# Attention: exchanging neighbouring partitions by transfers in place of two projections, and a later place for the tail's transposes, affinity and ranks

## The chip, the core and the metric

One core of one Trainium2 chip. The time is device microseconds for one execution of the whole program. The engines are PE (TensorE), ACT (ScalarE), DVE (VectorE), POOL (GpSimd) and SP (SyncE, which here only issues transfers). Each runs its own list of instructions in order; they meet at semaphores.

## The reference

The program is a chain of four layers over x [32, 256, 128]: attention with an MLP, a routed mixture of 8 experts, a selective scan and a rotation network. Only the first is touched. Cut to what matters (D = 128, 16 heads of 8):

```python
xn = _layernorm(x, ln1_g, ln1_b)
q = _l2norm((xn @ Wq).reshape(Bx, Tx, H, Dh))
k = _l2norm((xn @ Wk).reshape(Bx, Tx, H, Dh))
...
q = _rope(q, times)      # pairs: r1 = x1*cos - x2*sin, r2 = x1*sin + x2*cos
k = _rope(k, times)
gcp = jnp.exp(jnp.clip(jnp.cumsum(gj, axis=1), -60.0, 50.0))
q = q * gcp
k = k / (gcp + 1e-08)
...                      # p_exp, its cumulative sum p_cs
q = q / (p_cs + 1e-08)
k = k * p_exp
scores = jnp.einsum('bqhd,bkhd->bhqk', q, k) / math.sqrt(Dh)
attn = jax.nn.softmax(jnp.where(mask, scores, -jnp.inf), axis=-1)
...
# next layer's routing
aff = x @ centroids.T
eid = jnp.argmax(aff, axis=-1)
```

## The kernel before

Attention works on two sequences (512 tokens) at a time, 16 pairs, in software-pipelined steps k = -1 to 18. In one step four pairs are in flight: the layer norm of pair k+1 (`ln`), the projections of pair k (`front`), scores and softmax of pair k-1 (`scores`, its last quads `late` in the next step), and the MLP, routing and storing of older pairs (`mid`, `tail`). `tail` begins with step 3, `front` ends with step 15. The order of all work on each engine is written out by hand in `pe_step`, `act_step`, `dve_step`, `pool_step` and `sp_step`; nothing is reordered at run time.

*Projections.* Activations lie transposed, features on partitions, 512 tokens along the free axis. `project` is one fp32 product of 128x128 weights with `xt` into PSUM bank FA or FB. The rotary embedding needs each feature's neighbour (partition 2i with 2i+1). The kernel gets it by projecting a second time with the columns of the weights exchanged: `w_qs` beside `w_q`, `w_ks` beside `w_k`. DVE multiplies the one with `cos` (L812, L866), the other with `sin`, whose sign alternates by partition (L819, L861, into `rot_b`), and adds (L826, L918). The squares' sum over a head is a product with `ones_blk` (L481 for the query, L519 for the key).

*Scores.* `quad(n)` writes the scores of 4 heads into the four banks of RING, which exist once; it waits until `exps(n-1)` on ACT has read them. `exps(n)` writes `es`, which `weigh(n)` multiplies with V into the bank AV. `av_copy(i)` (ACT), `back(i)` (PE transposes), `heads_rec` and `heads_o` (DVE, L735 and L747) take each pair of weighs away:

```python
since(pe, s["s_exp"], u * 8 + n)        # in quad: RING is free
...
pe.wait_ge(s["s_exp"], u * 8 + n + 1)   # in weigh: es is there
```

*Tail.* DVE makes `xl2` (L762, four instructions) from the finished rows; PE transposes it (L352) into bank M, ACT copies it to `o_t` (L673), PE multiplies with the centroids (L507, the affinity), DVE derives the one-hot choice `hot`, and PE counts ranks from it (L535, L538) into FA, from which DVE takes `pos` and the slots. POOL scatters the rows. Bank M also serves the MLP.

*Clip and softplus.* POOL makes two products for the clock's softplus (L985 `f_lost`, L987 `f_soft`); DVE makes the cumulative sum `cum` (a scan, L858) and clips it (L863); ACT's `lgcp` (L679) needs the clip.

Of the kernel before, what the change touches and what calls it, by code (L numbers as in the profile page):

```python
# [80 lines left out]
def program(nc, dram, out):  # L81

    ctx = ExitStack()
    with ctx:
# [40 lines left out]
        for name, shape in (("w_a", [P, dram["w_a"].shape[1]]), ("w_1", [P, E * F]), ("w_2", [P, E * F])):  # L125
            c[name] = layer0.enter_context(nc.sbuf_tensor(name, shape, fp32))
# [10 lines left out]
        for name, width in W_A:  # L137
            c[name] = c["w_a"][:, at:at + width]
            at += width
# [28 lines left out]
def attention(nc, dram, d, c, banks):  # L168
# [18 lines left out]
    with ExitStack() as ctx:  # L187
# [4 lines left out]
            f_q f_qs f_sq f_ra f_rb f_rq f_ssq f_mq f_lq f_zq f_zq2 f_fq f_qt  # L192
            f_k f_ks f_sk f_ka f_kb f_rk f_ssk f_mk f_lk f_zk f_fk f_k1 f_k2 f_km f_v f_vaug
# [33 lines left out]
        rot_b = sb("rot_b", [P, STEP])  # L227
        factor = sb("factor", [P, STEP])
# [47 lines left out]
        of = sb("of", [1, ETILES])  # L276
        before = sb("before", [1, ETILES])
# [40 lines left out]

        def sp_step(sp, k, half, p, ln, front, scores, late, mid, tail):
# [18 lines left out]
            if front:  # L338

                sp.wait_ge(s["f_xlb"], one_on)  # L340
                sp.dma_start(rows(d["xlb"], here), xl[:, :, :]).then_inc(s["xlb_stored"], 16)


        def pe_step(pe, k, half, p, ln, front, scores, late, mid, tail):
# [171 lines left out]
            if front:  # L516
                pe.wait_ge(s["f_ka"], k + 1)
                pe.wait_ge(s["f_sk"], k + 1)
                pe.matmul(FB[:, :], c["ones_blk"], square[:, :], start=True, stop=True).then_inc(s["f_ssk"], 1)  # L519
            if scores:  # L520
                quad(3, k - 1, q)
            if mid:
# [5 lines left out]
                transposes(M, o_tok[p], s["m_ot"])  # L528
            if tail:
                pe.wait_ge(s["r_hot"], k - 2)  # L530
                if front:
                    pe.wait_ge(s["f_kb"], k + 1)
# [9 lines left out]
            if scores:  # L542
                weigh(2, k - 1, q)
                quad(4, k - 1, q)
# [9 lines left out]
            if front:  # L554
                pe.wait_ge(s["f_kb"], k + 1)
# [8 lines left out]
        def act_step(act, k, half, p, ln, front, scores, late, mid, tail):  # L564
# [106 lines left out]
            if tail:  # L671
                act.wait_ge(s["m_x2t"], k - 2)
                act.activation(o_t[:, :], M[:, :], ACT.Copy).then_inc(s["m_x2t_sb"], 1)  # L673
# [6 lines left out]
            if scores:  # L680
                av_copy(0, k - 1)
                exps(2, k - 1)
            if front:
# [40 lines left out]
        def dve_step(dve, k, half, p, ln, front, scores, late, mid, tail):  # L724
# [1930 lines left out]
```

## Time and profile before

| | |
|---|---|
| median of 3 runs | 2163.32 us (2157.25 to 2165.94) |
| the profiled execution, its span | 2164.4 us |
| attention, from the start of the span | about 780 us |
| PE busy in the span | 1849.2 us |
| DVE busy | 1703.8 us |
| ACT busy | 1474.7 us |
| POOL busy | 1165.1 us |

The span runs from the first to the last instruction of one profiled execution; no other time of that execution is on record, so the span stands for it. Busy times are of the whole program, whose later layers have other limits, so a step of attention has to be read in a timeline of its own.

### The profile page before, as it was taken

What the parts mean: (1) busy time and instruction counts of PE and PEld (TensorE: products, weight loads), DVE (VectorE), ACT (ScalarE), POOL (GpSimd) and SP (SyncE); (2) the same over time, 40 slices, a digit from 0 to 9 for tenths busy, and PEclk for the clock granted to TensorE, in tenths of its full rate; (3) what the DMA queues carried; (4) which work ended last, traced back from release to release, by engine and by line L of the source; (5) the groups of instructions that cost most, each with busy time, mean ns of one, the idle gap of its engine ahead of it and who ended that gap; (6) DMA issues with size and microseconds to landing.
All of it is one profiled execution on the core that took longest, in us unless ns stands there. A gap on an engine that the chain in (4) does not pass through costs nothing. (4 is left out here: it accounts for less than half of the span.)

```text
span 2164.4 us, 37241 instructions
## 1 busy us (share of the span) xinstructions
PE 1849.2 (85%) x12576; PEld 954.5 (44%) x12600; DVE 1703.8 (79%) x3547; ACT 1474.7 (68%) x2917; POOL 1165.1 (54%) x720
## 2 busy tenths in 40 slices
PE   6999999999998459957889889898898988659996
PEld 2566666656665259952222222222222222124453
DVE  7778868877863437854899999999999998976776
ACT  5888888888885138845656666666666666437775
POOL 2122232242221027871789999999999998840001
PEclk9999999999999669977899999999999998879998
DMA  4100010011001012221100111001111100023333
GB/s 169 36 26 26 28 49 26 26 36 41 21 25 33 20 50 77 88 72 42 30 25 27 34 35 34 27 30 30 31 35 35 35 31 30 21 67 90 97 84 78
DMA packets 103708, 97.35 MB, mean 45 GB/s; under 512 B 9137, under 2 KB 86113, under 8 KB 103137
## 3 DMA queue, kind: packets, MB, share of 16 engines
q1 hardware_dynamic: 95584, 75.34, 12.4%
q0 software_dynamic: 6784, 18.10, 2.5%
q8 instruction: 103, 1.69, 0.3%
q10 hardware_dynamic: 1152, 1.54, 0.2%
q14 instruction: 85, 0.69, 0.1%
HBM read 45.87 MB, written 28.10 MB: 34 GB/s over the span
## 5 line engine op out<-in xcount | busy, mean ns | idle before, releaser
L1935 POOL TENSOR_TENSOR hc<-h,c_rep 128x1024 f32<-128x1024 f32 x256 | 627.8, 2463 | 137.9 <-DVE h L1899 136.7
L1899 DVE TENSOR_TENSOR_SCAN h<-decay,bank 128x1024 f32<-128x1024 f32 x241 | 551.0, 2286 | 22.5 <-issue 0.9
L1757 ACT ACTIVATE decay<-bank,neg_a_r 128x510 f32<-128x510 f32 x512 | 322.6, 683 | 257.5 <-PE bank L1634 257.1
L1618 PE MATMUL bank<-u_in,sel_rows 32*128 32x512 f32 x964 | 287.9, 675 | 95.7 <-DVE h L1899 95.6
L1634 PE MATMUL bank<-delta,sel_rows 32*128 32x512 f32 x1024 | 338.8, 677 | 0.9 <-ACT decay L1757 0.9
L1886 DVE TENSOR_TENSOR bank<-bank,b_rep 128x1024 f32<-128x1024 f32 x241 | 291.2, 1208 | 34.8 <-PE bank L1618 33.0
L992 POOL DMA_INDIRECT rows_in_dram<-row,idx x64 | 63.3, 989 | 318.3 <-DVE row L965 303.7
L574 ACT ACTIVATE es<-bank 128x384 f32<-128x384 f32 x512 | 208.9, 499 | 22.1 <-PE bank L373 21.8
L1618 PEld LDWEIGHTS bank<-u_in,sel_rows 32*128 32x128 f32 x964 | 76.0, 191 | 276.7 <-DVE h L1899 199.7
L1649 PE MATMUL bank<-hc,y_sel 128*32 128x512 f32 x1024 | 149.6, 660 | 0.8 <-POOL hc L1935 0.8
L1656 PE MATMUL bank<-xpad,w_conv 128*128 128x512 f32 x256 | 133.0, 634 | 3.2 <-ACT xc L1819 1.6
L985 POOL TENSOR_TENSOR mag<-mag,front 128x512 f32<-128x512 f32 x16 | 21.4, 1335 | 194.6 <-ACT front L660 194.6
L2546 POOL DMA_DIRECT2D out_dram<-r_res x16 | 12.1, 759 | 209.9 <-DVE r_res L2413 202.0
L348 PE MATMUL bank<-xt,w_a 128*128 128x512 f32 x224 | 117.1, 608 | 7.9 <-DVE lnorm L915 3.8
L1634 PEld LDWEIGHTS bank<-delta,sel_rows 32*128 32x128 f32 x1024 | 99.9, 193 | 25.1 <-ACT decay L1757 18.2
L365 PE MATMUL bank<-q_t,k_m 32*128 32x256 f32 x1024 | 91.9, 428 | 2.3 <-ACT es L574 2.1
L387 PE MATMUL bank<-es,v_a 128*32 128x256 f32 x1024 | 81.4, 388 | 9.2 <-DVE o_tok L747 7.9
L418 PE MATMUL bank<-h_t,w_a 128*128 128x512 f32 x128 | 77.6, 690 | 13.1 <-ACT g L584 7.5
L1656 PEld LDWEIGHTS bank<-xpad,w_conv 128*128 128x128 f32 x256 | 43.2, 192 | 89.6 <-issue 83.6
L1350 POOL DMA_INDIRECT yx_dram<-yx,e_idx x72 | 70.2, 974 | 19.6 <-issue 16.4
L1299 PE MATMUL bank<-w,hid 128*128 x576 | 80.3, 283 | 0.0
L1287 PE MATMUL bank<-xst,w_tile 128*128 128x128 f32 x576 | 77.8, 279 | 1.7 <-issue 0.4
(341 smaller groups left out, 4170.0 us busy)
## 6 DMA issues: line engine op xcount, KB each, us to landing
r_tw<-r_o_t SPq DMA_DIRECT2D x96, 128.0 KB, 2.3
xvs<-xv SPq DMA_DIRECT2D x16, 512.0 KB, 2.9
u_wide<-u_rep_dram SPq DMA_DIRECT2D x30, 256.0 KB, 3.5
xs<-rows_in_dram SPq DMA_DIRECT2D x72, 68.0 KB, 1.8
front<-in_x_dram SPq DMA_DIRECT2D x16, 256.0 KB, 2.9
w<-in_w_dram SPq DMA_DIRECT2D x2, 2048.0 KB
xlb_dram<-front SPq DMA_DIRECT2D x16, 256.0 KB, 2.3
xlb_m<-xlb_dram SPq DMA_DIRECT2D x16, 256.0 KB
```

Source lines behind the costliest of these rows:

```text
L348: pe.matmul(bank[:, :], weight, xt[p][:, :], start=True, stop=True).then_inc(sem, 1)
L365: pe.matmul(RING[st][:, 0:T], kk[:, 0:P], qq, start=True, stop=True, tile_position=(32 * st, 0))
L387: pe.matmul(dst[:, col:col + T], v_a[par][:, 2 * b, HS * st + v, :], e[:, 0:T], start=True, stop=True, tile_position=(0, 32 * st))
L574: last = act.activation(es[(n % 2) * HS + st][:, :], RING[st][:, 0:3 * P], ACT.Exp, scale=DH ** -0.5)
L1618: last = pe.matmul(BD[n % 2][:, i * STEP:(i + 1) * STEP], sel[at:at + 32, r, :], u_in[p if n < NS else q][at:at + 32, hf, :], start=True, ...
L1634: pe.matmul(DL[i], sel[at:at + 32, r, :], delta[p if n < NS else q][at:at + 32, hf, :], start=True, stop=True, tile_position=(at, 0)).then ...
L1649: last = pe.matmul(Y[32 * st:32 * st + 32, :], c["y_sel"][:, r, :], hc[(2 * i + st // 2) % RING][:, st % 2, :], start=False, stop=r == 3, ...
L1656: last = pe.matmul(seq(G), c["w_conv"][:, tap, hf * P:(hf + 1) * P], xpad[:, :, tap:tap + T], start=tap == 0, stop=tap == TAPS - 1)
L1757: act.activation(decay[n % 4][:, i, :, 1:], seq(DL[i])[:, :, 1:], ACT.Exp, scale=c["neg_a_r"][:, hf, g:g + 1]).then_inc(s["n_da"], 1)
L1886: dve.tensor_tensor(pair_of(BD[n % 2]), pair_of(BD[n % 2]), b_rep[p if n < NS else q][:, :].unsqueeze(1).to_broadcast([P, 2, STEP]), ALU.m ...
L1899: dve.tensor_tensor_scan(flat(h[n % RING]), decay[n % 4].rearrange("p i b t -> p (i b t)"), flat(drive_0) if by_pool else BD[n % 2], 0.0, ...
L1935: pool.tensor_tensor(hc[n % RING][:, :, :], h[n % RING][:, :, :], c_rep[p if n < NS else q][:, :].unsqueeze(1).to_broadcast([P, 2, STEP]), ...
```

## The change

`w_qs` and `w_ks` and their two projections go. DVE multiplies the one projection with `cos` and with `sin`; the product with `sin` (`rot_b`) is then copied to `rot_s` with each pair of partitions exchanged, by two transfers of 64 partitions x 2 KB on SP's queue. As the alternating sign is taken before the exchange, the sum becomes a subtraction. The key's copy is ordered behind the query's (one `rot_s`). On DVE the query's subtraction moves from behind `centred(h_tok)` to behind `f_sp`, the key's product with `sin` to behind that with `cos`. On PE the query's `ones_blk` product moves between `weigh(6)` and `weigh(7)`, the key's projection behind `quad(0)`, the transposes of `xl2` behind `quad(2)`, the affinity behind the key's `ones_blk` product, the ranks behind `quad(4)`. On ACT the copy `o_t` of the transposes moves behind `exps(2)`. On DVE the work on `aff` and `hot` forms one run behind `heads_o(0)`, `pos` moves behind `q_t`. POOL's `f_lost` additionally waits for `m_xl2`. The weights `w_a` are loaded in three pieces without the two left out.

```diff
+        def swap(sp, sem):
+
+            for to in range(2):
+                sp.dma_start(rot_s[to:P:2, :], rot_b[1 - to:P:2, :]).then_inc(sem, 16)
...
# sp_step
             if front:
 
+                sp.wait_ge(s["f_rb"], one_on)
+                swap(sp, s["f_qsw"])
+                sp.wait_ge(s["f_kb"], one_on)
+                sp.wait_ge(s["f_rq"], one_on)
+                swap(sp, s["f_ksw"])
                 sp.wait_ge(s["f_xlb"], one_on)
...
# pe_step
             if late:
                 quad(7, k - 2, p)
-            if front:
-                pe.wait_ge(s["f_pe"], k + 1)
-                project(FB, c["w_qs"], s["f_qs"])
             if late:
                 weigh(6, k - 2, p)
+            if front:
+                pe.wait_ge(s["f_sq"], k + 1)
+                pe.wait_ge(s["f_rb"], k + 1)
+                pe.matmul(FA[:, :], c["ones_blk"], square[:, :], start=True, stop=True).then_inc(s["f_ssq"], 1)
+            if late:
                 weigh(7, k - 2, p)
...
                 quad(0, k - 1, q)
+            if front:
+                pe.wait_ge(s["f_pe"], k + 1)
+                project(FB, c["w_k"], s["f_k"])
             if late:
                 back(3, k - 2)
-            if front:
-                pe.wait_ge(s["f_sq"], k + 1)
-                pe.wait_ge(s["f_ra"], k + 1)
-                pe.matmul(FA[:, :], c["ones_blk"], square[:, :], start=True, stop=True).then_inc(s["f_ssq"], 1)
-                pe.wait_ge(s["f_rb"], k + 1)
-                project(FB, c["w_k"], s["f_k"])
...
-            if front:
-                pe.wait_ge(s["f_mq"], k + 1)
-                project(FA, c["w_ks"], s["f_ks"])
             if scores:
                 weigh(0, k - 1, q)
+            if scores:
+                weigh(1, k - 1, q)
+                quad(2, k - 1, q)
             if tail:
                 pe.wait_ge(s["m_xl2"], k - 2)
                 if ln:
                     pe.wait_ge(s["f_xt_sb"], k + 2)
                 transposes(M, xl2, s["m_x2t"])
-            if scores:
-                weigh(1, k - 1, q)
-                quad(2, k - 1, q)
-            if tail:
-                pe.wait_ge(s["m_x2t_sb"], k - 2)
-                for j in range(TS):
-                    last = pe.matmul(M[:, j * E:(j + 1) * E], o_t[:, j * P:(j + 1) * P], c["cent"][:, :], start=True, stop=True)
-                last.then_inc(s["m_aff"], 1)
             if scores:
                 back(0, k - 1)
...
             if front:
-                pe.wait_ge(s["f_ka"], k + 1)
+                pe.wait_ge(s["f_kb"], k + 1)
                 pe.wait_ge(s["f_sk"], k + 1)
                 pe.matmul(FB[:, :], c["ones_blk"], square[:, :], start=True, stop=True).then_inc(s["f_ssk"], 1)
+            if tail:
+                pe.wait_ge(s["m_x2t_sb"], k - 2)
+                for j in range(TS):
+                    last = pe.matmul(M[:, j * E:(j + 1) * E], o_t[:, j * P:(j + 1) * P], c["cent"][:, :], start=True, stop=True)
+                last.then_inc(s["m_aff"], 1)
             if scores:
                 quad(3, k - 1, q)
...
# the ranks (L535, L538) stand behind this now, no longer ahead of it
             if scores:
                 weigh(2, k - 1, q)
                 quad(4, k - 1, q)
...
# act_step
             if scores:
                 av_copy(0, k - 1)
                 exps(2, k - 1)
+            if tail:
+                act.wait_ge(s["m_x2t"], k - 2)
+                act.activation(o_t[:, :], M[:, :], ACT.Copy).then_inc(s["m_x2t_sb"], 1)
...
# dve_step
                 dve.tensor_tensor(seq(rot), seq(FA), cos, ALU.mult).then_inc(s["f_ra"], 1)
+                since(dve, s["f_ksw"], 32 * k)
+                dve.tensor_tensor(seq(rot_b), seq(FA), sin, ALU.mult).then_inc(s["f_rb"], 1)
...
                 dve.scalar_tensor_tensor(pre[:, 0, :], pre[:, 0, :], 0.0, log[:, 0, :], ALU.max, ALU.add).then_inc(s["f_sp"], 1)
+                dve.wait_ge(s["f_ra"], k + 1)
+                dve.wait_ge(s["f_qsw"], 32 * k + 32)
+                dve.tensor_tensor(rot[:, :], rot[:, :], rot_s[:, :], ALU.subtract).then_inc(s["f_rq"], 1)
...
                 dve.tensor_tensor(seq(rot_k), seq(FB), cos, ALU.mult).then_inc(s["f_ka"], 1)
+                dve.wait_ge(s["f_qsw"], 32 * k + 32)
+                dve.tensor_tensor(seq(rot_b), seq(FB), sin, ALU.mult).then_inc(s["f_kb"], 1)
...
+                dve.wait_ge(s["f_ksw"], 32 * k + 32)
+                dve.tensor_tensor(rot_k[:, :], rot_k[:, :], rot_s[:, :], ALU.subtract).then_inc(s["f_rk"], 1)
...
# pool_step
                 pool.wait_ge(s["f_back"], k + 1)
+                if tail:
+                    pool.wait_ge(s["m_xl2"], k - 2)
                 pool.tensor_tensor(mag[:, 1, :], mag[:, 1, :], one_up[:, :], ALU.subtract).then_inc(s["f_lost"], 1)
```

## Rows read from the trace of the kernel before

**Rows 1.** The page's busy times; the window view of one pass (length, then busy us).

```profile
PE 1849.2 (85%) x12576; PEld 954.5 (44%) x12600; DVE 1703.8 (79%) x3547; ACT 1474.7 (68%) x2917; POOL 1165.1 (54%) x720
...
310.60:352.40 41.80, 39.86 (x409) 26.23 (x408) 32.34 (x114) 36.04 (x78) 12.59 (x11) 1.00 0.11 33
```

**Rows 2.** Timeline of PE: start, length, line, operation, count, idle time before it.

```profile
294.51 0.66 PE L352 MATMUL bank<-consts,xl 128*128 128x128 f32 x4 [1.05 <-DVE xl L762]
...
325.77 1.02 PE L348 MATMUL bank<-xt,w_a 128*128 128x512 f32 x2
326.73 0.64 PE L387 MATMUL bank<-es,v_a 128*32 128x256 f32 x8
...
327.40 0.61 PE L387 MATMUL bank<-es,v_a 128*32 128x256 f32 x8
...
336.34 0.66 PE L352 MATMUL bank<-consts,xl 128*128 128x128 f32 x4 [1.05 <-DVE xl L762]
336.93 0.64 PE L387 MATMUL bank<-es,v_a 128*32 128x256 f32 x8
...
337.71 0.71 PE L365 MATMUL bank<-q_t,k_m 32*128 32x256 f32 x8
...
339.03 0.96 PE L507 MATMUL bank<-cent,o_t 128*128 128x8 f32 x8
...
341.27 0.71 PE L365 MATMUL bank<-q_t,k_m 32*128 32x256 f32 x8
...
343.16 0.19 PE L535 MATMUL bank<-hot,strict_b 128*128 128x32 bf16 x1
...
344.16 0.71 PE L365 MATMUL bank<-q_t,k_m 32*128 32x256 f32 x8
```

**Rows 3.** Timeline of ACT in the same pass: L580 is `av_copy`, L574 `exps`.

```profile
328.46 0.58 ACT L580 ACTIVATE avs<-bank 128x512 f32<-128x512 f32 x1
...
329.98 1.62 ACT L574 ACTIVATE es<-bank 128x384 f32<-128x384 f32 x4
...
333.56 1.62 ACT L574 ACTIVATE es<-bank 128x384 f32<-128x384 f32 x4
...
339.38 1.62 ACT L574 ACTIVATE es<-bank 128x384 f32<-128x384 f32 x4
...
342.45 1.64 ACT L574 ACTIVATE es<-bank 128x384 f32<-128x384 f32 x4 [0.27 <-PE bank L373]
```

**Rows 4.** Timeline of DVE in the same pass.

```profile
326.75 0.17 DVE L757 BATCH_NORM_AGGREGATE m_mean_var<-m_stats 128x2 f32<-128x6 f32 x1
...
327.04 0.66 DVE L819 TENSOR_TENSOR rot_b<-bank,consts 128x512 f32<-128x512 f32 x1
...
331.20 0.23 DVE L735 RECIPROCAL rec<-bank 128x16 f32<-128x16 f32 x1
...
333.01 3.28 DVE L762 TENSOR_SCALAR xl<-row,m_mean_var 128x128 f32<-128x128 f32 x4
...
337.92 0.41 DVE L863 TENSOR_SCALAR cum<-cum 128x512 f32<-128x512 f32 x1
```

**Rows 5.** Timeline of POOL in the same pass.

```profile
333.06 1.27 POOL L985 TENSOR_TENSOR mag<-mag,front 128x512 f32<-128x512 f32 x1 [11.72 <-ACT front L660]
```

**Rows 6.** Timeline of DVE in step 16, where POOL has no such product.

```profile
666.35 1.11 DVE L762 TENSOR_SCALAR xl<-row,m_mean_var 128x128 f32<-128x128 f32 x4
```

**Rows 7.** Timelines of DVE and of POOL in step 2.

```profile
82.97 1.23 DVE L858 TENSOR_TENSOR_SCAN cum<-consts,pre 128x512 f32<-128x512 f32 x1
...
85.81 1.10 DVE L863 TENSOR_SCALAR cum<-cum 128x512 f32<-128x512 f32 x1
...
83.38 1.88 POOL L985 TENSOR_TENSOR mag<-mag,front 128x512 f32<-128x512 f32 x1 [22.40 <-ACT front L660]
85.34 1.29 POOL L987 TENSOR_TENSOR log<-log,mag 128x512 f32<-128x512 f32 x1
```

**Rows 8.** Transfers of the last stage by line: issue us min/median/max, then time to landing.

```profile
L2103 SPq DMA_DIRECT2D r_tw<-r_o_t x48: 588/597/1064, 1946.5 to 2136.7; - x48
...
DMA to landing us min/median/max: 2.3/2.4/4.0
```

More of the change, by code:

```diff
@@ L124, in program @@
         layer0 = ctx.enter_context(ExitStack())
-        for name, shape in (("w_a", [P, dram["w_a"].shape[1]]), ("w_1", [P, E * F]), ("w_2", [P, E * F])):
+        for name, shape in (("w_a", [P, dram["w_a"].shape[1] - 2 * D]), ("w_1", [P, E * F]), ("w_2", [P, E * F])):
             c[name] = layer0.enter_context(nc.sbuf_tensor(name, shape, fp32))
@@ L227, in attention @@
         rot_b = sb("rot_b", [P, STEP])
+        rot_s = sb("rot_s", [P, STEP])
         factor = sb("factor", [P, STEP])
@@ L275, in attention @@
         end = sb("end", [1, E])
-        of = sb("of", [1, ETILES])
-        before = sb("before", [1, ETILES])
+        of, before = (log[0:1, 0, n * ETILES:(n + 1) * ETILES] for n in range(2))
         hi = sb("p_hi", [E * FC, P], bf16)
@@ L528, in pe_step @@
                 transposes(M, o_tok[p], s["m_ot"])
+            if scores:
+                weigh(2, k - 1, q)
+                quad(4, k - 1, q)
             if tail:
@@ L541, in pe_step @@
                 last.then_inc(s["r_rank"], 1)
-            if scores:
-                weigh(2, k - 1, q)
-                quad(4, k - 1, q)
             if mid:
@@ L815, in dve_step @@
                 bn_aggr(mv_m, stats_m, s["m_mv2"])
-            if front:
-                dve.wait_ge(s["f_qs"], k + 1)
-                since(dve, s["f_rk"], k)
-                dve.tensor_tensor(seq(rot_b), seq(FB), sin, ALU.mult).then_inc(s["f_rb"], 1)
             if tail:
@@ L822, in dve_step @@
                 centred(h_tok, x2, mv_m, rs_m, s["m_yn"])
-            if front:
-                dve.wait_ge(s["f_ra"], k + 1)
-                dve.wait_ge(s["f_rb"], k + 1)
-                dve.tensor_tensor(rot[:, :], rot[:, :], rot_b[:, :], ALU.add).then_inc(s["f_rq"], 1)
             if tail:
@@ L889, in dve_step @@
                 dve.scalar_tensor_tensor(factor[:, :], lnorm[:, :], -0.5, cum[:, :], ALU.mult, ALU.subtract).then_inc(s["f_zq"], 1)
+            if scores:
+                heads_o(0, k - 1, q)
+            if tail:
+                dve.wait_ge(s["m_aff"], k - 2)
+                dve.tensor_copy(aff[:, :, :], M[:, 0:TS * E].rearrange("p (j e) -> p j e", j=TS)).then_inc(s["m_aff_sb"], 1)
+                dve.wait_ge(s["m_aff_sb"], k - 2)
+                dve.tensor_reduce(best[:, :], aff[:, :, :], AX.X, ALU.max).then_inc(s["r_dve"], 1)
+            if tail:
+                dve.wait_ge(s["r_dve"], 9 * k - 26)
+                dve.tensor_tensor(hot_f[:, :, :], aff[:, :, :], best[:, :].unsqueeze(2).to_broadcast([P, TS, E]), ALU.is_ge).then_inc(s["r_dve"], 1)
             if tail:
@@ L896, in dve_step @@
                 dve.tensor_reduce(first[:, :], hot_f[:, :, :], AX.X, ALU.max).then_inc(s["r_dve"], 1)
-            if scores:
-                heads_o(0, k - 1, q)
             if tail:
@@ L906, in dve_step @@
                 dve.tensor_tensor(factor[:, :], factor[:, :], pcs[:, :], ALU.subtract).then_inc(s["f_zq2"], 1)
+            if front:
+                dve.wait_ge(s["f_ssk"], k + 1)
+                dve.wait_ge(s["f_zq"], k + 1)
+                dve.tensor_scalar(lnorm[:, :], FB[:, :], 1e-24, None, ALU.max).then_inc(s["f_mk"], 1)
+                dve.wait_ge(s["f_ka"], k + 1)
+                dve.wait_ge(s["f_ksw"], 32 * k + 32)
+                dve.tensor_tensor(rot_k[:, :], rot_k[:, :], rot_s[:, :], ALU.subtract).then_inc(s["f_rk"], 1)
+                dve.wait_ge(s["f_fq"], k + 1)
+                dve.wait_ge(s["f_rq"], k + 1)
+                since(dve, s["s_score"], 32 * k - 32)
+                dve.tensor_tensor(q_t[p][:, :], rot[:, :], factor[:, :], ALU.mult).then_inc(s["f_qt"], 1)
             if tail:
@@ L984, in pool_step @@
                 pool.wait_ge(s["f_back"], k + 1)
+                if tail:
+                    pool.wait_ge(s["m_xl2"], k - 2)
                 pool.tensor_tensor(mag[:, 1, :], mag[:, 1, :], one_up[:, :], ALU.subtract).then_inc(s["f_lost"], 1)
```

48 lines of the change are left out of this document (13 added, 35 removed).

## The prediction

> **What bounds the kernel now.** I read the page first: TensorE (PE) is the busiest engine of the whole span [rows 1]. The change touches only attention, so the second view is the timeline of one steady pass there. Its landmark, the four transposes of `xl2`, comes at 294.51 and again at 336.34 [rows 2]: a pass takes 41.83 us, and the thirteen passes from step 3 to step 15 repeat it to 0.01 us. In it PE is busy 39.86 us, ACT 36.04, DVE 32.34 [rows 1]. So PE looks like the bound, with one visible hole of 1.05 us where it waits for DVE's `xl2` [rows 2]. The obvious sum is then two projections (0.96 us each, 325.77 to 326.73) and that hole, 2.97 us a pass.
>
> The rows say that this is not the whole chain. PE is in lockstep with ACT: `quad(n)` may not overwrite RING before `exps(n-1)` has read it, and `weigh(n)` needs `exps(n)`. A quad's scores release `exps` 1.18 us after the quad starts (341.27 to 342.45) and `exps` takes 1.62 to 1.64 us; `exps(3)` ends at 342.45 + 1.64 = 344.09 and `quad(4)` starts at 344.16 [rows 2, 3]. A quad can start only some 2.89 us after the one before, whatever PE is spared. So I follow the pass of 320 to 352 piece by piece, both engines and DVE, in the order of the changed code. Work that is not named keeps its durations.
>
> **Step 1, the query's projection goes and its normaliser comes early.** `quad(7)` ends at 325.77. Now `weigh(6)` follows 0.96 us earlier, to 326.44. Next in PE's queue is the `ones_blk` product, which now waits for `f_rb`. DVE's `rot_b` starts at 327.04 today, behind the aggregate of 326.75 [rows 4]; in its new place ahead of it, it starts at 326.75 and ends 0.66 later, at 327.41. PE stalls 1.02 us, the product takes about 0.90 (an estimate just under a projection of the same shape), and `weigh(7)` starts at 328.36 where it was at 327.40 [rows 2]: +0.96. Behind it on ACT is `av_copy(3)`, in order, at 328.46 [rows 3] and now, when `weigh(7)` has ended, at 329.25 (an estimate: its 0.78 and a hand-over); `exps(0)` follows 1.52 behind as today, from 329.98 to 330.77, +0.79. The removed projection has bought a stall of its own size, and the product that was moved is the delay. `quad(1)` has to wait for `exps(0)`: 330.77 + 1.64 + 0.07 = 332.48.
>
> **Step 2, the key's projection goes.** ACT runs without a gap from `exps(0)` to `exps(1)`, 3.58 us (329.98 to 333.56) [rows 3], so `exps(1)` starts at 334.36 and ends at 335.98. PE now has nothing between `weigh(0)` and `weigh(1)` and stands 1.55 us, until 336.05. `weigh(1)` takes 0.78 (336.93 to 337.71), then `quad(2)` starts at 336.83, was 337.71 [rows 2]: here 0.88 us is ahead.
>
> **Step 3, DVE, POOL and the port.** `back(3)` now stands behind the key projection, so DVE's `rec` moves from 331.20 to 331.98 [rows 4] (+0.78), and the query's sum `rot - rot_s`, moved behind it, adds 0.60. `xl2` starts at 333.01 + 1.38 = 334.39. Today it takes 3.28 us, since POOL's `f_lost` product starts 0.05 us later and runs beside it [rows 4, 5]; where POOL is idle the same four take 1.11 [rows 6]. POOL will now wait for `m_xl2`, so it ends at 335.50, 0.79 earlier. But the two POOL products then start just as DVE's scan `cum` starts. Steps 0 to 2 show that collision: the scan at 82.97 ran 1.23 to 84.20, the POOL product issued at 83.38 lasted 1.88 and ended 1.06 behind the scan, and the clip, issued at 85.81 beside the second POOL product, ended 0.28 behind that (86.91) instead of after 0.41 [rows 7]. In the new pass: scan 335.43 to 336.66, first POOL product to 337.72, clip to 338.00. Without the collision the clip would end at 337.1. It ends at 338.33 today [rows 4], so 0.33 is left of the gain. It feeds ACT's `lgcp`, which stands in front of `av_copy(0)` and `exps(2)`: `exps(2)` from 339.38 to 339.05 [rows 3], ending 340.67.
>
> The page "SBUF — State Buffer" of the Trainium skill, section "Who interferes with whom", has a rule for this: a DVE instruction with two SBUF inputs, or in a 2-port mode, and a GpSimd instruction that reads SBUF exclude each other, the first to start holding the pair to its end. It speaks against the change: by it the collision is certain, and the forecast's sum holds; without it the sum would be that of the rival "no collision" below. The trace agrees in steps 0 to 2 and shows nothing of it for this pair in the steady pass.
>
> **Step 4, the tail's transposes, affinity and ranks.** The `xl2` transposes no longer wait. Their copy `o_t` now follows `exps(2)` on ACT: 340.53 to 341.11 (a 128x512 copy takes 0.58 [rows 3]). The affinity needs it and starts at 341.16; it takes 0.96 [rows 2], of which some 0.15 lies beside the next instruction (an estimate), and `quad(3)` starts at 341.97, was 341.27: +0.70. So the affinity, formerly ahead, now stands in the lockstep. `exps(3)` 343.15 to 344.79, `quad(4)` 344.86 (+0.70). The ranks now come behind it, 0.22 (343.16 to 344.16 less `weigh(2)`'s 0.78) [rows 2]; before they filled the wait for `exps(3)`. `quad(5)` is late by 0.9, then `exps(5)`, `k_m` and `h_t`, which are in that order on ACT, and through `h_t` the next pass. DVE's part (`hot` now in one dependent run, `pos` behind the ranks) ends about 1 us late too and holds `weigh(4)`, but the next pass is set by ACT's +0.9.
>
> **Step 5, the four transfers a pass.** SP's other four issues of a pass wait for `f_xn`, `m_x1`, `m_y1` and `f_xlb`, none of which falls due between the swaps and their users, so the queue is free (where `xlb_dram` is stored late, POOL alone waits for it). Nearest row: the 128 KB twists of the last stage, 0.60 us of issue and 2.4 us to landing [rows 8], two in a row about 3 us after the operand is ready. The query's is ready at 327.41 and wanted at 333.71; the key's at 339.16 and wanted at 344.92. Each has some 3 us to spare: cost nothing; each microsecond of landing beyond 5.7 would cost one. The stride of two partitions is not in the trace; I bound a transfer between 2.4 and its longest there, 4.0 [rows 8], and both hide. The weights come in three pieces instead of one at the start, hidden behind the constants. DVE's count of large instructions is unchanged.
>
> **Sum.** 13 steady passes (3 to 15) at +0.9: 11.7. Step 16 has no projections and no transfers, but the affinity behind `exps(2)`: +1.3. Steps 0 to 2 have no `xl2`; the late `rot - rot_s` moves the scan from before to behind POOL's product, and step 0 also waits for its transfer: I take an estimate of +1.0 each, between 0 and +2 (the clip's 0.7 lost to a collision today [rows 7], once or twice more): 3. Together +16.0 on the profiled execution, whose trace spans 2164.4 us; that is 1.1 above the median of the three runs, which becomes 2163.3 + 16.0 = 2179 us.
>
> **The rivals.**
> *As worked out*, 2179: chance 0.50. Its own range, from the neglected hand-over times (0.05 to 0.1 each, some six in the chain, so ±0.5 a pass), is 2171 to 2188.
> *No collision*: scan and POOL product run side by side. `exps(2)` starts at 338.1, the copy and affinity make it `quad(3)` at 341.1, 0.2 early, and the ranks take it back: 0.0 a pass, +4 in all, 2167. For it: rows 7 are of other passes. Against it: they are the same two instructions. 0.22.
> *PE is the bound after all*, the other side: ACT's order gives way and the stalls before `ones_blk` (1.02) and `weigh(1)` (1.55) do not appear. Then 2.97 a pass is saved, 39 us, 2124. For it: PE's 39.86 of 41.8. Against it: `exps(0)` to `exps(1)` has no gap on ACT. It decides if PE's idle time a pass falls below the present 2 us. 0.12, with cases halfway (2145).
> *POOL takes the port first*: its semaphore comes 0.05 us behind a scan that starts 0.07 before `xl2` ends. If POOL wins, the scan waits a whole product, the clip comes 1.2 later still: +2.1 a pass, 27 + 4.3, 2195. 0.10.
> *A swap lands late*, from 5.7 us on: at 7 us +1.3 more a pass, 2196. 0.06.
>
> **How the numbers follow.** A measurement of this kernel tells about 0.5% from no change, 10.8 us: below 2152.5 is faster, above 2174.1 slower. Slower: most of the first (0.44) and of the last two (0.15), 0.59 together. Same: 0.06 of the first, 0.18 of "no collision", 0.03 elsewhere, 0.27. Faster: 0.11 and a strip of "no collision", 0.14. The range reaches from 2150, leaving out most of the third case, to 2197, which holds the last two where they just begin: 0.15 to 0.2 outside.
>
> **What would show it.** Right: PE idle of about 1.0 before the first `ones_blk` product and 1.5 before `weigh(1)`; busy PE down by 1.9 to about 38 and a pass of 42.7; `xl2` in 1.1 us; POOL's first product near 2.2 us and a clip of 1.3; `quad(3)` behind the affinity; no DVE wait on `rot_s`. Wrong: a pass under 41.8, a clip of 0.41, or DVE idle at `rot - rot_s`. The forecast falls if ACT reaches `exps(1)` sooner after `exps(0)` than 3.58 us, or if `quad(3)` is not held by the affinity.

## The result, and the profile after

| | before | changed |
|---|---|---|
| median of 4 runs each | 2162.13 us | 2191.73 us (2185.43 to 2197.31) |
| span of the profiled execution | 2164.4 us | 2195.5 us |
| a steady pass | 41.83 us | 43.19 us |
| start of the experts' stage | 784.78 us | 812.78 us |

The ratio is 1.014 with an interval of 1.0118 to 1.0161: slower, on the predicted side and in the range, but by 30 us where 16 were forecast. All but 3 us of the 31 by which the two spans differ has arisen when the experts' stage starts, so it lies in attention.

I followed one landmark there, the start of the down-projection (L460 before, L472 after): steps 0 to 2 cost 9.7 us (step 3 has it at 121.22, was 111.52), thirteen passes cost 1.36 each, 17.6, step 16 costs 1.3, and the rest gives back 0.6. Together 28.0. The two terms that are far off are the first (forecast 3) and the second (forecast 11.7).

The page's busy times, and the window of one pass as in [rows 1] (length, then busy of PE, its weight loads, DVE, ACT, POOL):

```profile
PE 1840.4 (84%) x12536; PEld 948.6 (43%) x12536; DVE 1701.4 (77%) x3547; ACT 1475.8 (67%) x2917; POOL 1176.5 (54%) x720
...
337.17:380.36 43.19, 38.91 (x403) 25.66 (x403) 31.97 (x113) 36.13 (x78) 13.42 (x12) 1.00 0.14 44
```

PE is busy 0.95 us less in a pass and the pass is 1.36 us longer; DVE and ACT are about as busy as they were. The granted clock is 1.00 in both windows, the upper level of 2.4 GHz. So the pass is not longer by more work: somebody waits. PE's timeline of that pass, against [rows 2]:

```profile
344.05 1.10 PE L482 MATMUL bank<-square,consts 128*128 128x512 f32 x2 [0.84 <-DVE rot_b L822]
345.07 0.64 PE L399 MATMUL bank<-es,v_a 128*32 128x256 f32 x8
...
352.69 0.64 PE L399 MATMUL bank<-es,v_a 128*32 128x256 f32 x8 [1.22 <-ACT es L582]
...
353.48 0.71 PE L377 MATMUL bank<-q_t,k_m 32*128 32x256 f32 x8
...
354.80 0.60 PE L364 MATMUL bank<-consts,xl 128*128 128x128 f32 x4
...
357.93 1.06 PE L526 MATMUL bank<-cent,o_t 128*128 128x8 f32 x8 [0.49 <-ACT o_t L690]
358.92 0.71 PE L377 MATMUL bank<-q_t,k_m 32*128 32x256 f32 x8
...
361.79 0.71 PE L377 MATMUL bank<-q_t,k_m 32*128 32x256 f32 x8 [0.17 <-ACT es L582]
...
363.11 0.18 PE L546 MATMUL bank<-hot,strict_b 128*128 128x32 bf16 x1
```

The old wait of 1.05 before the `xl2` transposes (L364) is gone. In its stead PE waits for `rot_b` before the `ones_blk` product, for `es` before `weigh(1)`, and for `o_t` before the affinity. ACT, as in [rows 3]:

```profile
346.00 0.60 ACT L588 ACTIVATE avs<-bank 128x512 f32<-128x512 f32 x1 [0.38 <-PE bank L403]
...
347.53 1.62 ACT L582 ACTIVATE es<-bank 128x384 f32<-128x384 f32 x4
...
351.02 1.62 ACT L582 ACTIVATE es<-bank 128x384 f32<-128x384 f32 x4
...
354.75 0.63 ACT L684 ACTIVATE lgcp<-cum 128x512 f32<-128x512 f32 x1 [1.10 <-DVE cum L865]
...
355.76 1.62 ACT L582 ACTIVATE es<-bank 128x384 f32<-128x384 f32 x4
357.25 0.63 ACT L690 ACTIVATE o_t<-bank 128x512 f32<-128x512 f32 x1
...
360.10 1.64 ACT L582 ACTIVATE es<-bank 128x384 f32<-128x384 f32 x4 [0.88 <-PE bank L385]
```

From `exps(0)` to `exps(1)` it still has no gap (3.49 us). DVE, as in [rows 4]:

```profile
343.22 0.68 DVE L822 TENSOR_TENSOR rot_b<-bank,consts 128x512 f32<-128x512 f32 x1
...
344.71 1.11 DVE L770 TENSOR_SCALAR h_tok<-x,m_mean_var,m_rstd 128x128 f32<-128x128 f32 x4 [0.51 <-ACT m_rstd L641]
...
348.68 0.26 DVE L743 RECIPROCAL rec<-bank 128x16 f32<-128x16 f32 x1 [0.80 <-PE bank L411]
...
350.44 0.69 DVE L853 TENSOR_TENSOR rot<-rot,rot_s 128x512 f32<-128x512 f32 x1
...
351.12 1.11 DVE L770 TENSOR_SCALAR xl<-row,m_mean_var 128x128 f32<-128x128 f32 x4
352.14 1.22 DVE L863 TENSOR_TENSOR_SCAN cum<-consts,pre 128x512 f32<-128x512 f32 x1
353.40 1.32 DVE L865 TENSOR_SCALAR cum<-cum 128x512 f32<-128x512 f32 x1
```

and POOL, as in [rows 5]:

```profile
352.37 2.06 POOL L990 TENSOR_TENSOR mag<-mag,front 128x512 f32<-128x512 f32 x1 [14.49 <-DVE xl L770]
```

`xl2` takes 1.11 instead of 3.28, and the collision has moved to the scan, POOL's product and the clip, which takes 1.32 instead of 0.41. The sum `rot - rot_s` does not wait. The transfers of `rot_s`, by line, as in [rows 8]:

```profile
L324 SPq DMA_DIRECT2D rot_s<-rot_b x64: 464/564/989, 23.0 to 658.8; - x64
...
  DVE rot L853: 0.2, 1
...
DMA to landing us min/median/max: 1.9/2.1/3.8
```

In 64 transfers DVE waited once, for 0.2 us.

### The profile page after: what moved, and what is told of

Same layout as the page of the kernel before. It is cut to its first block and busy times, and to the rows that moved or that the text cites. A ratio compares the mean times of both kernels' runs of the same rounds, so it can differ in the third digit from the quotient of the medians.

```text
span 2195.5 us, 37201 instructions
## 1 busy us (share of the span) xinstructions
PE 1840.4 (84%) x12536; PEld 948.6 (43%) x12536; DVE 1701.4 (77%) x3547; ACT 1475.8 (67%) x2917; POOL 1176.5 (54%) x720
## 5 line engine op out<-in xcount | busy, mean ns | idle before, releaser
L990 POOL TENSOR_TENSOR mag<-mag,front 128x512 f32<-128x512 f32 x16 | 30.9, 1931 | 235.2 <-DVE xl L770 187.2
L360 PE MATMUL bank<-xt,w_a 128*128 128x512 f32 x160 | 85.7, 624 | 5.5 <-ACT v_a L601 3.3
L385 PE MATMUL bank<-mask_b,ident_b 128*128 128x256 bf16 x512 | 79.0, 277 | 0.0
```

Source lines behind the costliest of these rows:

```text
L360: pe.matmul(bank[:, :], weight, xt[p][:, :], start=True, stop=True).then_inc(sem, 1)
```

## The experiments

A pass is told as the distance of two down-projections in the steady stretch. The first four kernels ran on one chip; a second chip took the next four and a third the last four. On those two the ten passes from step 4 to step 13 are some 1.45 us longer than on the first, at one place that has nothing to do with the edits (last section); the pass told is that of these steps. So passes are compared within a chip: the changed kernel has 43.19 us in its first measurement (whose chip is not on record, but the kernel with the projections back has the same 43.19 on the first) and 44.67 on the third. It was not run on the second; there the kernel with doubled transfers, at 44.66, is taken for it (reasons below). Ratios are to the kernel before on the same chip.

**PE's time handed back.** The two projections return as products that nobody reads, at their old places in PE's order; the rest is the changed kernel.

```diff
             if late:
                 quad(7, k - 2, p)
+            if front:
+                pe.wait_ge(s["f_pe"], k + 1)
+                pe.matmul(FB[:, :], c["w_q"], xt[p][:, :], start=True, stop=True)
...
                 quad(1, k - 1, q)
+            if front:
+                pe.wait_ge(s["f_mq"], k + 1)
+                pe.matmul(FA[:, :], c["w_k"], xt[p][:, :], start=True, stop=True)
```

> The changed kernel with two projections of the size of those removed (128x512) put back at their old places on PE, with no reader: one behind quad(7), one behind quad(1). Theory A (the changed pass is set by waits for f_rb, exps(1) and the clip, so TensorE time there is worth nothing): both lie in PE's waits, 0.84 us in front of the ones_blk product and 1.22 in front of weigh(1); the pass stays at 43.19 us within 0.15 and the time within 0.2% of the changed kernel. Rival B (PE is the bound, and removing the projections did save): 1.9 us a pass more, +25 to +30 us.

Measured: 2192.46 us, ratio 1.0149 (1.0109 to 1.0188), pass 43.19. PE is 21 us busier over the whole and not a hundredth of a steady pass is lost: the wait before `ones_blk` is gone, that before `weigh(1)` shrank to 0.36. In this order, what the change takes off PE is worth nothing. PE's busy time in a pass is 40.62 here, where the same work had 39.86 before the change.

**The tail's work back.** The `xl2` transposes, the affinity and the ranks on PE, the copy `o_t` on ACT, and DVE's `aff`, `hot` and `pos` go back to their old places; exchange, `ones_blk` and key projection stay.

> The changed kernel with the tail's transposes, affinity, ranks, the copy o_t and DVE's small steps at the places of the kernel before; the transfers stay. Theory A (the affinity behind exps(2), 0.98 us, and the ranks, 0.2, stand in the lockstep of quads and exps): quad(3) goes back to directly behind exps(2), about 1.45 us earlier, the pass falls from 43.19 to 41.6 to 41.9 us, the time by 17 to 21 us, back to within 0.5% of the kernel before. Rival B (the exchange by transfers is what costs): the pass stays above 42.8. Rival C: the xl2 wait of 1 us comes back and eats half, pass 42.5.

Measured: 2176.93, ratio 1.0086 (1.0057 to 1.0115), pass 42.40. The late tail costs 0.79 a pass, more than half of the loss, but the pass didn't fall to the 41.6 to 41.9 of theory A; it lies nearest to rival C (42.5), whose wait for `xl2` is there. DVE has no gap behind `rec(3)` here, and PE now waits 0.81 for `xl2` and 0.85 for `hot`:

```profile
341.61 1.10 PE L482 MATMUL bank<-square,consts 128*128 128x512 f32 x2 [0.84 <-DVE rot_b L822]
...
349.84 0.66 PE L364 MATMUL bank<-consts,xl 128*128 128x128 f32 x4 [0.81 <-DVE xl L770]
...
357.77 0.19 PE L543 MATMUL bank<-hot,strict_b 128*128 128x32 bf16 x1 [0.85 <-DVE hot L905]
```

**The query's normaliser later.** The changed kernel with the `ones_blk` product behind `quad(0)`.

```diff
             if late:
                 weigh(6, k - 2, p)
-            if front:
-                pe.wait_ge(s["f_sq"], k + 1)
-                pe.wait_ge(s["f_rb"], k + 1)
-                pe.matmul(FA[:, :], c["ones_blk"], square[:, :], start=True, stop=True).then_inc(s["f_ssq"], 1)
...
                 quad(0, k - 1, q)
+            if front:
+                pe.wait_ge(s["f_sq"], k + 1)
+                pe.wait_ge(s["f_rb"], k + 1)
+                pe.matmul(FA[:, :], c["ones_blk"], square[:, :], start=True, stop=True).then_inc(s["f_ssq"], 1)
```

> The changed kernel with the query's ones_blk product behind quad(0) instead of between weigh(6) and weigh(7). Theory A1 (the clip is what exps(2) waits for, and it hangs on back(3)): exps(0) and quad(1) come about 0.5 us earlier, but exps(2) hardly moves; the pass changes by 0 to -0.35 us, time -5 us or less. Theory A2 (the stall before ones_blk is the delay that is carried to the end of the pass): pass -0.8 us or more, time -10 us or more.

Measured: 2182.9, ratio 1.0108 (1.0069 to 1.0148), pass 42.79: 0.40 less. That lies between the two theories (0 to 0.35, and 0.8 or more). `exps(0)` comes 0.48 earlier after the down-projection (9.88 us, was 10.36), DVE waits 0.39 before `rec(3)` instead of 0.80, and the clip comes 0.40 earlier.

**Only POOL's wait.** The kernel before, with the one line of `pool_step`.

```diff
                 pool.wait_ge(s["f_back"], k + 1)
+                if tail:
+                    pool.wait_ge(s["m_xl2"], k - 2)
```

> The kernel before with one edit: POOL's f_lost product also waits for m_xl2. Theory A (xl2 is slowed by POOL beside it, and the hole of 1.05 us on PE is that): xl2 takes 1.1 us instead of 3.28, the hole goes, the collision moves to scan and clip (POOL product 2.1, clip 1.3) where it costs less; pass 41.83 to about 41.0, time -8 to -12 us. Rival B: the clip's delay eats all of it, same or slower.

Measured: 2148.17 where the kernel before has 2160.91, ratio 0.9943 (0.9925 to 0.9961), pass 40.77. One line gives 1.06 us a pass. In DVE's timeline `xl2` is short and the clip grows only from 0.41 to 0.86, since `rot_b` stands between scan and clip:

```profile
327.85 1.11 DVE L762 TENSOR_SCALAR xl<-row,m_mean_var 128x128 f32<-128x128 f32 x4
328.88 1.22 DVE L858 TENSOR_TENSOR_SCAN cum<-consts,pre 128x512 f32<-128x512 f32 x1
330.01 0.67 DVE L861 TENSOR_TENSOR rot_b<-bank,consts 128x512 f32<-128x512 f32 x1
330.59 0.86 DVE L863 TENSOR_SCALAR cum<-cum 128x512 f32<-128x512 f32 x1
```

**More of the order back.** The tail's work as above, and also `back(3)`, `ones_blk` and the key's projection in the order of before.

> The exchange by transfers in nearly the order of the kernel before: tail work at its old places, and on PE quad(0), back(3), the query's ones_blk product, the key's projection, as before. What is left of the change: no second projections, the transfers, the query's subtraction behind f_sp, the m_xl2 wait. Theory A (from DVE's rec, L743, to the end of the pass DVE has no idle time and sets the pass, so what delays rec or stands behind it counts in full): rec comes back by about 1.0 us, the subtraction's 0.6 stays; pass 40.77 (kernel before with the m_xl2 wait) + 0.6 = 41.4 us, time 0.2 to 0.6% under the kernel before. Rival B (the transfers cost something themselves): pass above 41.9. Rival C (PE is the bound here and two projections less pay): pass below 40.5.

Measured on the second chip: 2212.62, ratio 1.001 (0.9994 to 1.0027), pass 42.90, which less 1.47 is 41.43. The pass is as expected, the whole is not (0.2 to 0.6% faster was): the down-projection of step 3 comes at 119.01, so the gain of the passes is lost in steps 0 to 2.

**The query's sum earlier.** The changed kernel with `rot - rot_s` ahead of `rec(3)` instead of behind `f_sp`.

> The changed kernel with the query's subtraction rot - rot_s moved from behind f_sp to ahead of DVE's rec (L743), where DVE stands idle 0.80 us. Theory A: the transfer has landed by then (ready at 343.9, landed near 347.0, wanted at 347.9 in the frame of the pass at 344 us), the 0.60 us falls into idle time; xl2, clip and exps(2) come 0.6 earlier, pass 43.19 to 42.6, time -7 us. Rival B (the transfer is late there): DVE waits on rot_s, pass unchanged or longer.

Measured: 2227.15, ratio 1.0076 (1.0053 to 1.0099), pass 44.08, 0.58 less than the 44.66 taken for the changed kernel on that chip: the sum's 0.60 was on the path, and in its earlier place it fills DVE's wait of 0.80 before `rec(3)`. In the first steps it now comes before its transfer has landed: DVE waited four times, 9.8 us together.

**POOL's products behind the clip.** The changed kernel, with POOL waiting for `f_clip` in place of `m_xl2`.

> The changed kernel with POOL's two softplus products waiting for the clip instead of xl2, so that they collide with neither. Theory A: clip 0.41 us instead of 1.32 and exps(2) about 0.9 earlier, but the products end later (2.65 us behind the clip), DVE waits for them at f_sp1, about 0.6 later than now, and DVE sets the pass: 43.1 to 43.5 us, no gain. Rival B (the collision is what costs, through exps(2)): pass 42.3 to 42.5, -9 us or more.

Measured: 2248.66, ratio 1.0175 (1.014 to 1.021), pass 45.05, 0.39 slower than the 44.66 taken for the changed kernel; three passes are longer still (46.26, 46.31, 47.56), which I haven't followed. The clip is short, but DVE's second softplus now waits 1.61 for POOL's second product; what follows on DVE comes late, and the transposes of `o_tok` wait 1.00 us for `aff`, whose bank they need.

**Twice the transfers.** Ahead of each pair, two more of the same size to an unused place in memory.

```diff
+            for dst, to, w in ((d["rot_x"], 0, STEP), (d["rot_x"], 1, STEP), (rot_s, 0, STEP), (rot_s, 1, STEP)):
+                sp.dma_start(dst[to:P:2, :], rot_b[1 - to:P:2, 0:w]).then_inc(sem, 16)
```

> The changed kernel with twice as many transfers: ahead of each pair two more of the same size, from rot_b to a DRAM scratch that nobody reads, and the users wait for all four. Each exchange lands about 1.1 to 1.5 us later. Theory A (the transfers have 2 to 3 us to spare in a steady pass): pass stays at 43.19 within 0.1; only steps 0 and 2, where the wait is tight, lose about 1 us each; +1 to +4 us. Rival B (the exchange's latency is in the pass): +1.1 us or more a pass, +15 to +30 us.

Measured: 2237.69, ratio 1.0115 (1.0079 to 1.0151), pass 44.66. The changed kernel has ratios of 1.014 and 1.0133 on the other two chips and 44.67 on the third, with the same hold-up of 1.36 us a pass, so another 1.1 us on the queue ahead of each pair changes nothing in the steady pass; 1.1 a pass more would be 45.8. The comparison runs across chips. In the filling steps DVE waits for it twice, 2.4 us together.

**Without POOL's wait.** The changed kernel less that line.

> The changed kernel without POOL's wait for m_xl2: the products are free to start as soon as one_up is there. In the changed kernel that is at 350.45 us of the span, beside the sum rot - rot_s (350.44) and 0.7 us ahead of xl2 (351.12). Theory: POOL's first product then takes the port from xl2, which takes about 3.3 us again instead of 1.11, as in the kernel before; the scan starts about 2 us later, the clip is short or stretched by the second product, and exps(2) and the affinity follow: the pass is 44.3 to 45.3 us against 43.19, the wait is the one part of the change that helps, and the whole is 15 to 25 us slower than the changed kernel. Rival: in the new order the wait only moves the collision from xl2 to the scan and the clip, at no gain: pass 43.0 to 43.4. Third: the wait costs, since both products come later: pass under 43.0.

Measured on the third chip: 2255.02, ratio 1.0211 (1.0184 to 1.0237), pass 45.83 where the changed kernel has 44.67 beside it: +1.16. POOL's product starts beside `rot - rot_s` (362.96), and DVE's small instruction before `xl2` and `xl2` itself both stand behind it:

```profile
362.87 0.69 DVE L853 TENSOR_TENSOR rot<-rot,rot_s 128x512 f32<-128x512 f32 x1
363.47 1.24 DVE L856 SCALAR_TENSOR_TENSOR row<-m_mean_var,row 128x8 f32<-128x8 f32 x1
364.63 2.07 DVE L770 TENSOR_SCALAR xl<-row,m_mean_var 128x128 f32<-128x128 f32 x4
366.62 1.21 DVE L863 TENSOR_TENSOR_SCAN cum<-consts,pre 128x512 f32<-128x512 f32 x1
367.86 0.43 DVE L865 TENSOR_SCALAR cum<-cum 128x512 f32<-128x512 f32 x1
```

From the start of `rot - rot_s` to the end of the clip this takes 5.42 us, with the wait 4.28 (350.44 to 354.72): the difference of 1.14 is nearly that of the passes.

**The exchange alone, with POOL's wait.** As "more of the order back", and DVE's `rot_b` back behind the aggregate.

```diff
             if front:
                 dve.wait_ge(s["f_sq"], k + 1)
                 dve.tensor_tensor(seq(rot), seq(FA), cos, ALU.mult).then_inc(s["f_ra"], 1)
-                since(dve, s["f_ksw"], 32 * k)
-                dve.tensor_tensor(seq(rot_b), seq(FA), sin, ALU.mult).then_inc(s["f_rb"], 1)
             if tail:
                 dve.wait_ge(s["m_st2"], k - 2)
                 bn_aggr(mv_m, stats_m, s["m_mv2"])
+            if front:
+                since(dve, s["f_ksw"], 32 * k)
+                dve.tensor_tensor(seq(rot_b), seq(FA), sin, ALU.mult).then_inc(s["f_rb"], 1)
```

> The exchange by transfers and POOL's wait, with all else in the order of the kernel before: the tail's transposes, affinity and ranks, back(3), the ones_blk product behind it, the key's projection behind that, and DVE's rot_b behind the aggregate. Only rot - rot_s stands at its new place, behind f_sp, since the transfers have to land. Theory: DVE's chain from the end of the down-projection to the clip has the same number of instructions of the same size as in the kernel before with POOL's wait, and no gap: pass 40.7 to 41.0, as there (40.77). The exchange then is worth nothing in the steady pass, and the whole loss of 1.4 a pass is the new order. The late rot - rot_s in steps 0 to 2 still costs, the down-projection of step 3 starts at 115 to 119 us instead of 111.7: whole 2150 to 2157 where the kernel before takes 2161. Rival: the transfers themselves delay (landing, or the port of the tile's partitions): DVE idle at rot - rot_s in the steady pass, and 41.5 or more.

The query's sum and, with only one projection to read, the key's product with `sin` keep their new places.

Measured: 2204.75, ratio 0.9974 (0.9956 to 0.9992), pass 42.34, down-projection of step 3 at 117.45. In the steady pass it is 0.13 behind the kernel before with the wait, on the same chip. The gap of 0.51 that the changed kernel has before `h_tok` is gone: there the aggregate stands behind `rot_b` and reaches ACT's `m_rstd` 0.6 later.

**The last two, beside them.** The kernel before with POOL's wait, and the changed kernel.

> The kernel before with POOL's wait for m_xl2 and nothing else, once more beside the others on one chip: pass 40.8 us, down-projection of step 3 at 111.7 us, 0.5 to 0.7% faster than the kernel before. Rival: a difference of chips, ratio within 0.3% of 1.

> The changed kernel, not altered, beside the others on one chip: pass 43.2 us, down-projection of step 3 at 121.2 us, 1.4% slower than the kernel before. If this chip also holds PE up by 1.5 us a pass ahead of the up-projection, as the last one did, 44.7.

Measured: 2194.89, ratio 0.9935 (0.9912 to 0.9958), pass 42.21, step 3 at 111.55; and 2239.48, ratio 1.0133 (1.0105 to 1.0161), pass 44.67, step 3 at 122.59. Both ratios repeat those of the first chips. The fastest of all versions is the kernel before with one more wait.

From these a sum for the steady pass:

| step | us a pass | from |
|---|---|---|
| before | 41.83 | |
| POOL's wait | -1.06 | 41.83 to 40.77, first chip |
| the exchange in the old order | +0.13 | 42.21 to 42.34, third chip |
| the new order | +2.33 | 42.34 to 44.67, third chip |
| changed | 43.23 | read: 43.19 |

The new order in parts, with 1.47 taken off what ran on the second chip and 1.44 off the third: the tail's work 0.79 (43.19 to 42.40), `back(3)`, `ones_blk` and the key's projection 0.97 (to 41.43), `rot_b` ahead of the aggregate 0.53 (to 40.90).

And for steps 0 to 2, on the third chip: the exchange in the old order 5.9 us (111.55 to 117.45), the new order 5.1 more (to 122.59). These steps repeat less well than the passes: the changed kernel has 121.22 on the first chip and 122.59 on the third, so the 122.74 with the tail back and the 122.96 with the later `ones_blk`, both on the first, tell little.

## Why the prediction was right, and where it was not

**The number.** The side and the mechanism of the steady pass were right, the size was not. The forecast gave its own chain 2171 to 2188; the measured 2191.7 lies above that, and inside the whole range only because this reached to 2197 for two rivals that the traces refute. That it holds the number is luck in that part.

**The chain.** Every wait that it worked out is in the trace, in order. Shifted by 16.48 us (the distance of the two down-projections, 320.69 and 337.17), the profile after reads against the forecast:

| | forecast | read | late by |
|---|---|---|---|
| `ones_blk` starts | 327.46 | 327.57 | 0.11 |
| `weigh(7)` | 328.36 | 328.59 | 0.23 |
| `exps(0)` | 330.77 | 331.05 | 0.28 |
| `exps(1)` | 334.36 | 334.54 | 0.18 |
| `quad(2)` | 336.83 | 337.00 | 0.17 |
| `xl2` | 334.39 | 334.64 | 0.25 |
| clip ends | 338.00 | 338.24 | 0.24 |
| affinity | 341.16 | 341.45 | 0.29 |
| `quad(3)` | 341.97 | 342.44 | 0.47 |
| `quad(4)` | 344.86 | 345.31 | 0.45 |

(The forecast 327.46 is `weigh(6)`'s end of 326.44 and the stall of 1.02.) The error is made at two places. At the first, `rot_b` to `weigh(7)`, 0.23: the hand-over from DVE to PE takes 0.15 where the sum has 0.05, and `weigh(7)` starts 1.02 behind the product and not 0.90. At the second, the affinity holds `quad(3)` for 0.99 and not 0.81: I let 0.15 of it lie beside the next instruction, and its eight products took 1.06 and not 0.96. Together 0.41, with 0.05 between them, and the pass has 1.36 where 0.9 was forecast. The mechanism was right and two terms of step 1 and step 4 were undersized; "±0.5 a pass" for neglected hand-overs was about the true size, but they all have the same sign. (The stall before `ones_blk` is 0.84 and not 1.02, since `weigh(6)` ends later than forecast; the stall ends when `rot_b` is there either way.)

Three signs came otherwise than named. PE's busy time fell by 0.95 to 38.91 and not by 1.9 to 38: in the new order the same work counts as 0.76 more (40.62 against 39.86, with the projections back), since a product beside a wait overlaps its neighbours less, `ones_blk` with 1.10 where it had 1.02. The pass is 43.19 and not 42.7. And `exps(1)` comes 3.49 after `exps(0)`, 0.09 sooner than the 3.58 below which the forecast was to fall; that moved the chain by the 0.09 and no more.

**Step 1, the query's projection.** Right in kind: "the removed projection has bought a stall of its own size, and the product that was moved is the delay". With the projection back the pass is the same. With the product moved it falls by 0.40, half of the 0.79 that this step charged to `exps(0)`, which itself comes only 0.48 earlier.

**Step 2.** Right. ACT has 3.49 us without a gap between `exps(0)` and `exps(1)`, and PE waits 1.22 there.

**Step 3, the port.** Right in the end: POOL's first product runs into the scan and the clip takes 1.32. But how much the wait is worth was understated. I compared only the clip's end with today's and found 0.33; against the same order without the wait it is 1.16, and in the old order 1.06. In the old order it decides the sign: the exchange with it has a pass of some 40.9 us, below the 41.83 of before, and without it would be near 42.0 (an estimate: the 1.06 added; that kernel wasn't run). The rule of the Trainium skill that the prediction weighed ("SBUF — State Buffer", section "Who interferes with whom") is borne out in the steady pass too: a DVE instruction of 8 columns from two SBUF inputs lasts 1.24 us beside POOL's product where it takes 0.16. The scan of `pre` takes 1.22 when it is first and 2.28 when POOL's product is.

**Step 4, the tail.** Right: the affinity in the lockstep is the larger part, 0.79 a pass with what hangs on it. What I didn't see is that DVE stands just behind: with the tail back, the pass falls only to 42.40, since `rec(3)`, behind the key's projection, and `rot - rot_s` have filled DVE's chain. Putting more of the order back took another 0.97 (42.40 to 41.43, across chips), and moving the sum alone took 0.58 from the changed kernel. I had named both delays (+0.78, +0.60) and then let ACT alone set the pass. Nothing of the forecast hung on that, but a reader who would mend the kernel from my chain would have stopped halfway.

**Step 5, the transfers.** Right. Landing 2.1 us, below the nearest row's 2.4, one wait of 0.2 us, and twice as many change nothing in the steady pass.

**The rivals.** "No collision" is refuted by the clip of 1.32, "PE is the bound" by the experiment that hands PE its time back, "POOL takes the port first" by the scan of 1.22, "a swap lands late" by the waits.

**The step that failed: steps 0 to 2.** "I take an estimate of +1.0 each, between 0 and +2", 3 in all; it was 9.7, the largest miss of the sum. I looked there only for the clip and POOL. DVE's `pmax` (L791 before, L799 after) falls once in each of these steps and divides them; beside each length stands the granted TensorE clock of the stretch:

| | before | changed | longer by |
|---|---|---|---|
| ahead of step 0 | 18.44 | 19.00 | 0.56 |
| step 0 | 25.50 (0.93) | 29.87 (0.89) | 4.37 |
| step 1 | 29.65 (1.00) | 32.17 (0.89) | 2.52 |
| step 2 | 34.25 (1.00) | 36.49 (1.00) | 2.24 |

DVE in these steps:

```profile
24.21 0.69 DVE L848 TENSOR_SCALAR lnorm<-bank 128x512 f32<-128x512 f32 x1 [1.28 <-PE bank L482]
...
25.72 1.46 DVE L853 TENSOR_TENSOR rot<-rot,rot_s 128x512 f32<-128x512 f32 x1 [0.22 <-DMA rot_s<-rot_b]
27.10 2.28 DVE L863 TENSOR_TENSOR_SCAN cum<-consts,pre 128x512 f32<-128x512 f32 x1
...
62.81 0.69 DVE L868 TENSOR_TENSOR rot_k<-bank,consts 128x512 f32<-128x512 f32 x1 [4.32 <-ACT square L678]
...
89.83 0.26 DVE L743 RECIPROCAL rec<-bank 128x16 f32<-128x16 f32 x1 [4.77 <-PE bank L411]
```

and PE at the two `ones_blk` products of step 0 and the query's of step 1:

```profile
23.08 1.10 PE L482 MATMUL bank<-square,consts 128*128 128x512 f32 x2 [2.99 <-DVE rot_b L822]
...
31.97 2.08 PE L522 MATMUL bank<-square,consts 128*128 128x512 f32 x2 [3.48 <-DVE rot_b L870]
...
52.92 2.04 PE L482 MATMUL bank<-square,consts 128*128 128x512 f32 x2 [3.23 <-DVE rot_b L822]
```

In step 0 no quads and no tail fill the queues, so the chain is bare: projection, `rot`, `rot_b`, `ones_blk`, `lnorm`, the sum, scan. The product waits for `rot_b`, since both products of the query now read bank FA, which `ones_blk` overwrites; before, `rot_b` read FB, and PE waited 0.18 there. DVE has nothing to do meanwhile (1.28). The key's `ones_blk` (L522) waits 3.48 for `rot_b` in the same way, where it waited 0.59. The sum, formerly in that hole, stands in front of the scan, beside POOL. The scan itself takes 2.28 as it did in this step before; the forecast's "from before to behind POOL's product" holds in step 2 alone, where it takes 2.30 and took 1.23. In step 1 `ones_blk`, now ahead of `quad(0)`, holds PE and with it the scores for 3.23 us, and DVE waits 4.32 behind ACT; in step 2 it waits 4.77 for `back(3)`, where it waited 1.43. And the clock is lower: behind PE's idle stretches of 3.48 and 3.23 us it is granted the lower level of 1.2 GHz for a time in steps 0 and 1, where the products above take 2.08 and 2.04 instead of 1.10; before, step 1 ran at 1.00 throughout. The sum has no such term.

The exchange alone, in the old order, shows part of it in step 1: DVE waits 1.28 for the product and 2.14 for the transfer, and the scan takes 2.29 where it took 1.23 in the kernel before with the wait.

```profile
53.88 0.69 DVE L849 TENSOR_SCALAR lnorm<-bank 128x512 f32<-128x512 f32 x1 [1.28 <-PE bank L491]
...
57.31 0.70 DVE L854 TENSOR_TENSOR rot<-rot,rot_s 128x512 f32<-128x512 f32 x1 [2.14 <-DMA rot_s<-rot_b]
57.94 2.29 DVE L864 TENSOR_TENSOR_SCAN cum<-consts,pre 128x512 f32<-128x512 f32 x1
```

These waits are shown; how the 9.7 us divide among them and the clock is not. A transfer that is hidden in every steady pass may be on the path where the pipeline fills.

**Step 16** was forecast at 1.3 and measured at 1.3. The mechanism is there: PE waits 1.02 for `o_t` ahead of the affinity, and `quad(3)` comes 1.47 later after the down-projection. That the number agrees to a tenth is in part luck, for the granted clock falls within this step, sooner or later: the same kernel takes 43.65 us for it on the first chip at a mean clock of 0.92 and 44.97 on the third at 0.89, and the one with the projections back 45.12 at 0.89.

## What to carry to other kernels

Taking work off the busiest engine of a pipelined loop is worth what the pass shortens, and that is found by following who releases whom: here, in the changed order, the two projections could be left out or put back with the steady pass the same to the hundredth. Such an edit frees a place in the order, and the instructions that move into it are the cost, so each has to be tried alone, above all one that now stands between two links of the binding lockstep. The filling steps of a pipeline need a working of their own, since little there covers a wait, and behind PE's idle time the granted clock was lower here as well; and an operand's bank with a second reader makes the next writer wait for both.

## What the runs showed of the hardware

*Two chips hold most passes up at one place.* From step 4 to step 13, in all eight kernels that ran on the second and third chips and in none on the first, ACT stands idle 1.3 to 1.5 us before `h_t`, though the transposes that release it have ended by the profile, and DVE's next read of a projection waits 1.31 instead of 0.49. In the two passes after, some 0.6 is left of it. ACT's timeline of the changed kernel on the third chip, and of it with the returned projections on the first:

```profile
334.83 0.78 ACT L597 ACTIVATE h_t<-bank,vec 128x512 f32<-128x512 f32 x1 [1.37 <-remote]
```

```profile
370.22 0.76 ACT L603 ACTIVATE h_t<-bank,vec 128x512 f32<-128x512 f32 x1
```

PE's next product waits 1.65 instead of 0.17; for one and the same kernel, the one before with POOL's wait, the pass is 1.44 longer (40.77 and 42.21). The kernel before took 2210.8 us there and 2160.9 on the first chip, 2.3% apart, while the ratios of the changed kernel agree (1.014 and 1.0133). This place is only a third of it: of the 46.8 us between the spans of the kernel with POOL's wait (2143.1 and 2189.9), 15.8 have arisen at the last down-projection and 31 more arise in the experts' stage behind it. The cause is open; I made no run for it. A pass read on one chip can't be set against one from another before a kernel common to both has been read.

*A transfer of 64 partitions x 2 KB with a stride of two partitions* in SBUF on either side lands in 2.1 us (1.9 to 3.8) and takes SP 0.56 to issue: no slower than the transfers of [rows 8], which have no stride (2.4 and 0.60).

*A short instruction can be held as long as a long one.* The 128x8 operation that starts 0.51 us behind POOL's product (362.96, 1.72 long) ends at 364.71, 0.03 behind it, and so lasts 1.24 us instead of 0.16; the 128x512 clip of the changed kernel lasts 1.32 instead of 0.41 in the same way.
